# Two recurrent blocks stepped inside the expert slots of the first layer, and the shared expert's last two blocks moved into the second layer's slots

## The chip, the cores and the metric

The kernel runs on one core of one Trainium2 chip. The metric is device time in microseconds (us), the median of the runs shown. Engines: PE (TensorE), DVE (VectorE), ACT (ScalarE), POOL (GpSimd) and SP (SyncE), which here issues most of the DMAs.

## The reference, cut to what matters

`x` has 32 sequences of 128 steps of 128 values, 4,096 tokens. Two layers follow one another, each with a residual sum:

```
z  = polynomial(x, side inputs)                     # per token
x1 = x  + moe0(z)      # 8 experts, top 2, hidden 256, exact gelu, biases
h_t = tanh(x1_t @ Wx + b + h_(t-1) @ Wh)            # 128 steps, one after another
x2 = x1 + shared_swiglu(h) + moe1(h)   # 8 experts, top 2, hidden 256, gates from layernorm(h)
```

All in float32. The recurrence runs over the 128 steps for all 32 sequences at once.

## The kernel before

**Blocks.** Tokens are cut into NB = 8 blocks of 16 steps x 32 sequences (512 tokens, NT = 4 tiles of 128). Each engine has its own instruction stream, written out by hand; order within an engine is program order, and semaphores join the engines.

**Routing of layer 0** goes in five groups of blocks (`GROUPS`). POOL sends each token's row, with its gate and its place, to a region per expert in DRAM (`scatter0`). DVE makes two tables of slots: a first one, of `FULL_SLOTS[0]` = 32 slots that are surely full once the groups up to `CUT` = 2 are counted, and a second with the rest of the 71 slots (`find_blocks`, `sum_table`, `write_table`).

**Slots of layer 0** (`slots0`). A slot is 128 rows of one expert. SP loads its rows from DRAM into a ring of 18 (`slot_rows`; row r waits for the result of slot r-17). In slot j PE does, in this order: transpose rows j+3 (`turn_rows`), the hidden product of j (`hidden_slot`), transpose the activations of j-3 (`turn_act`), and the down product of j-5 (`slot_down`). ACT copies the two transposes and does the gelu; DVE adds the bias and gates the result (`add_bias`, `gate_result`); POOL sends the result rows to DRAM (`send_result`). Each of the four PSUM targets (`up_ps`, `turned_ps`, `act_turned_ps`, `result_ps`) has two banks, used in turn. SP then loads the results back, a block at a time, one after another (`parts`, L466); DVE adds two halves and `x` (`add_one`, `sum_x1`) and gets x1 of the block.

**The recurrent stream** (`stream_body(i)`, i = 0 to 7). Body i does the 16 steps of block i (`rnn_step` on PE, `tanh_step` on ACT) and, between the steps, the work behind block i-1: rows of h transposed and copied for routing (`state_rows`, `copy_rows`), the shared expert (`pair`, `silu`, `multiply`, `down1`), router logits, choice, gates (DVE). In step 10 PE transposes x1 of the next block (`turn_back`) and in steps 13 and 14 multiplies it by Wx (`rnn_input`). The ranks of block i-2 are counted at step 1, and POOL sends its rows from then on, at steps set by `scatter_step`. Body 0 has no block behind it; PE is filled with unused products (`FILL`, `keep_warm`). DVE splits the expert weights into a high and a low part there (`split_wgu`).

**Slots of layer 1** (`slots1`). Four shared slots (`SHARED_SLOTS`) carry the shared expert of block 7, then 71 expert slots follow: the first 40 from table 2, which needs blocks 0 to 5 sent; the other 31 from table 3, which needs all blocks sent. Routing of block 7 is laid between the slots of DVE by `POST_AT`. POOL's queue is: for block 6 eight sends, with the inverse deviation of block 7 (`inv_std`) after three of them; then one result a slot, and the eight sends of block 7 before the results of slots 8 to 15 (`SCATTER_AT`). At the end the result rows are loaded and summed (`add_parts`) and stored.

Of the kernel before, what the change touches and what calls it, by code (L numbers as in the profile page):

```python
# [36 lines left out]
P = 128  # L37
# [9 lines left out]
NG, GT = len(GROUPS), max(len(g) for g in GROUPS) * NT  # L47
# [12 lines left out]
SPLIT = 6  # L60


CUT = 2
ALL_SLOTS, FULL_SLOTS = TOPK * TOK // P + E - 1, (32, 40)
# [5 lines left out]
SHARED_SLOTS = NT  # L70
# [15 lines left out]
for _name, _size in (("ident", P), ("tri", P), ("ones", P), ("center", P), ("ramp", E), ("region", E), ("ids", TOK // P * TOPK),  # L86
                     ("dest", max(LAYER_SLOTS)), ("full", TOK // P), ("whole", TOK // P), ("upto", 4 * E * E), ("slot", max(WIDE)), ("power", NT), ("pad", ROW)):
    CONSTS[_name] = slice(sum(s.stop - s.start for s in CONSTS.values()),
                          sum(s.stop - s.start for s in CONSTS.values()) + _size)
# [11 lines left out]
FILL = [{s: 2 for s in range(STEPS) if s not in (TURN_X1_AT, *XP_AT)}, {1: 2}, {1: 2}] + (NB - 4) * [{}] + [{1: 2, 10: 2}]  # L101
# [3 lines left out]
VAR_STEP = 4  # L105
ONE_AT = {0: (1,), 1: (4,)}, {0: (2, 3), 2: (5,), 3: (6,), 4: (7,)}


def scatter_step(m):

    last = m - (SPLIT - 1) * NT * TOPK
    return 2 * STEPS + 3 + 2 * m if last < 0 else STEPS * (NB - 1) + 1 + 3 * last // 2
# [22 lines left out]
FIRST_X1_AT, FIRST_TURN_AT = 66, ALL_SLOTS + 3  # L135
HELD_ROWS = ALL_SLOTS // ROWS_RING * ROWS_RING + -(-BLK // ROW)
# [6 lines left out]
LAST_STD_BEHIND = 3  # L143


def b_use(n):
    return 2 * n
# [21 lines left out]
def tiles_of(layer, n):  # L169

    return NT if layer else len(GROUPS[n]) * NT


def tiles_on(layer, q, n):

    return sum(tiles_of(layer, m) for m in range(n) if m % (2 + layer) == q)
# [36 lines left out]
def build(nc, consts, x, fside_BxS_0, cond_1024, L0_cond_coeffs, L0_ffn_Wg, L0_ffn_bg, L0_ffn_W1, L0_ffn_b1,  # L213
# [5 lines left out]
    with ExitStack() as ctx:  # L219
# [33 lines left out]
        up_ps, result_ps = banks[:, 0:2, :], banks[:, 2:4, :]  # L253
        turned_ps, act_turned_ps = banks[:, 4:6, :], banks[:, 6:8, :]
# [3 lines left out]
        def rank_ps(layer, n):  # L258
            return bank_b if layer == 0 else turned_ps[:, RANKS_ROW % 2, :] if n == NB - 1 else bank_c
# [7 lines left out]
        last_logits = sb("last_logits", [P, NT * E])  # L267
# [25 lines left out]
        def temporaries(d):  # L293
            buf = work[:, 0, :] if d >= 2 else stream[:, :]
# [9 lines left out]
        stats, moments = sb("stats", [P, NT, 6]), sb("moments", [P, NT, 2])  # L304
        var, rstd = sb("var", [P, NT]), sb("rstd", [P, NT])
        hrows = [hrow0, hrow1]
        ids = const["ids"].rearrange("p (n t k) -> p n t k", n=NB, k=TOPK)
        poss = [[sb(f"pos{k}{q}", [P, (GT, NT)[k], TOPK], U32) for q in range(2 + k)] for k in range(2)]
        pos_f = sb("pos_f", [P, GT, TOPK])
        choices, new_choices = sb("choices", [P, E]), sb("new_choices", [P, E])  # L310
        before = [sb(f"before{q}", [P, NT, E]) for q in range(2)]
# [5 lines left out]
        rows = [next(carve(buf, (ROWS_RING, ROW))) for buf in (hT[:, BLK:], wgu)]  # L317
# [42 lines left out]
        def counted_after(layer, n):  # L360
            return layer and {SPLIT - 1: 1, NB - 1: 2}.get(n)
# [17 lines left out]
        def _(sp):  # L379
# [12 lines left out]
            def slot_rows(d, middle=lambda: None):  # L392
# [65 lines left out]
            slot_rows(1)  # L458
            for n in range(NB):
                if n == 0:  # L460
                    results_landed(0, DONE[0])
                elif n == GROUPS[CUT][-1] + 1:
                    results_landed(0, LAYER_SLOTS[0])
                if n:
                    sp.wait_ge(parts0_in, 16 * n)
                sp.dma_start(parts[:, n, :, :], result_rows[0][n]).then_inc(parts0_in, 16)  # L466
# [1176 lines left out]
```

## Time and profile before

| what | us |
|---|---|
| median of 3 runs (456.72 to 459.83) | 458.12 |
| the profiled execution, device time | 460.27 |
| its span in the profile | 458.5 |
| PE busy / POOL busy / DVE busy in the span | 404.3 / 282.4 / 337.9 |
| granted TensorE clock, mean share of full speed | 0.909 |

The span is what the trace covers; 1.8 us of the device time lie around it. A group of instructions is named by engine, line of the kernel and operands: `L1258` is the helper `mm` that issues every matmul, `L1262` the helper `turn` that issues blocks of transposes, so these are told apart by their operands. `PEld` is the load of weights into the array, which overlaps the products. In brackets stands how long the engine sat idle before and what released it; "issue" means nothing that the profile shows.

### The profile page before, as it was taken

The numbers are of one execution on the slowest core, as the hardware profiler recorded it, in microseconds if no ns is written. First come the engines' busy times: TensorE is split into PE (matmuls) and PEld (weight loads), VectorE is DVE, ScalarE is ACT, GpSimd is POOL, SyncE is SP. The second block draws the span as 40 slices with busy tenths as digits, with TensorE's granted clock in tenths as the row PEclk, the third lists the DMA queues.
The fourth block names the chain that finished last, engine by engine and source line by source line (L and its number), as shares of the span: only waits on it lengthen the run. The fifth ranks groups of instructions, "written<-read, shape, count | busy, mean of one in ns | idle before, by whom it ended". The sixth has DMA issues, their size and how long they took to land.

```text
span 458.5 us, 10143 instructions
## 1 busy us (share of the span) xinstructions
PE 404.3 (88%) x2428; PEld 328.4 (72%) x2428; DVE 337.9 (74%) x1299; ACT 206.4 (45%) x660; POOL 282.4 (62%) x289
## 2 busy tenths in 40 slices
PE   3699889677999999999999999998886999999950
PEld 3376555565899999966878888875675888888840
DVE  4687878388788888883767776888679777667782
ACT  1111304131777777744454554453433455555520
POOL 0536767677777777773146666665445677776670
PEclk9977766557999999999899999998989999999995
DMA  5996111115454444642101111112412353333757
GB/s 146 273 319 213 52 46 54 48 54 126 131 134 109 110 110 108 196 141 87 68 24 37 43 41 36 47 36 76 103 47 70 83 147 96 100 97 84 277 163 211
DMA packets 48150, 49.79 MB, mean 109 GB/s; under 512 B 8627, under 2 KB 37246, under 8 KB 47966
## 3 DMA queue, kind: packets, MB, share of 16 engines
q1 hardware_dynamic: 38680, 30.46, 24.9%
q0 software_dynamic: 8640, 17.84, 11.7%
q10 hardware_dynamic: 774, 0.84, 0.6%
q8 instruction: 23, 0.38, 0.3%
q14 instruction: 33, 0.27, 0.2%
HBM read 27.99 MB, written 21.12 MB: 107 GB/s over the span
## 4 chain that ended last, share of the span: by engine, by line
PE 70%; DVE 16%; DMA 6%; issue 5%; POOL 1%; SPq 1%; ACT 1%; DVEq 0%; POOLq 0%; ACTq 0%
PE banks L1258 58%; PE banks L1262 9%; DMA parts<-results 4%; PE banks L1347 3%; POOL results L541 1%; DMA base<-in_x 1%; DVE stream L802 1%; DVE stream L798 1%; DVE state_lo L1131 1%; DVE stream L796 1%; DVE y_row L1040 1%; DMA results<-y_row,y_dest 0%; DVE stream L793 0%; DVE act_row L1138 0%; DVE rt_d L851 0%
## 5 line engine op out<-in xcount | busy, mean ns | idle before, releaser
L541 POOL DMA_INDIRECT results<-y_row,y_dest x142 | 139.8, 984 | 61.9 <-issue 31.7
L508 POOL DMA_INDIRECT regions<-first_w,pos x64 | 62.1, 971 | 46.7 <-ACT hT L641 29.9
L508 POOL DMA_INDIRECT regions<-parts,pos x64 | 64.2, 1003 | 32.2 <-issue 32.2
L641 ACT ACTIVATE hT<-banks,pcol 128x32 f32<-128x32 f32 x128 | 36.9, 288 | 54.1 <-PE banks L1258 52.6
L623 ACT COPY act_col<-banks 128x256 f32<-128x256 f32 x146 | 54.1, 370 | 10.8 <-PE banks L1262 10.1
L700 ACT ACTIVATE silu_row<-banks 128x256 f32<-128x256 f32 x75 | 28.8, 384 | 63.2 <-PE banks L1258 63.2
L1262 PE MATMUL banks<-const_sb,act_row 128*128 128x128 f32 x292 | 56.6, 276 | 0.0
L1258 PEld LDWEIGHTS banks<-hT,wh 128*128 128x128 f32 x256 | 40.0, 191 | 23.0 <-ACT hT L641 19.4
L1262 PEld LDWEIGHTS banks<-const_sb,act_row 128*128 128x128 f32 x292 | 41.6, 143 | 19.0 <-issue 1.6
L1138 DVE TENSOR_TENSOR act_row<-silu_row,banks 128x256 f32<-128x256 f32 x75 | 31.5, 421 | 29.3 <-ACT silu_row L700 25.9
L1258 PE MATMUL banks<-hT,wh 128*128 128x32 f32 x256 | 50.4, 279 | 0.0
L1258 PE MATMUL banks<-first_w,state 128*128 x142 | 43.7, 391 | 2.0 <-DVE silu_row L1025 1.6
L1258 PE MATMUL banks<-wd,act_col 128*128 x284 | 44.1, 278 | 1.0 <-DVE y_row L1040 1.0
L1258 PE MATMUL banks<-first_w,act_col 128*128 x284 | 43.8, 277 | 0.4 <-ACT act_col L623 0.3
L1258 PE MATMUL banks<-hT,sw_raw 128*128 128x256 f32 x112 | 39.0, 431 | 0.0
L1258 PEld LDWEIGHTS banks<-wd,act_col 128*128 128x128 f32 x284 | 37.7, 193 | 1.4 <-issue 1.3
L1258 PEld LDWEIGHTS banks<-first_w,act_col 128*128 128x128 f32 x284 | 37.3, 191 | 1.3 <-issue 1.2
L617 ACT ACTIVATE act_row<-silu_row 128x256 f32<-128x256 f32 x71 | 29.6, 417 | 14.1 <-DVE silu_row L1025 10.7
L1258 PE MATMUL banks<-parts,xpow 96*128 96x512 f32 x48 | 35.3, 897 | 0.0
L1258 PE MATMUL banks<-wgu_hi,state_hi 128*128 x71 | 34.5, 486 | 0.7 <-issue 0.3
L1025 DVE TENSOR_TENSOR silu_row<-banks,first_w 128x256 f32<-128x256 f32 x71 | 29.7, 419 | 5.9 <-issue 3.7
L1258 PE MATMUL banks<-wgu_hi,state_lo 128*128 x71 | 28.4, 400 | 0.0
(191 smaller groups left out, 831.7 us busy)
## 6 DMA issues: line engine op xcount, KB each, us to landing
parts<-results SPq DMA_DIRECT2D x16, 512.0 KB, 5.6
hT<-regions SPq DMA_DIRECT2D x71, 65.0 KB, 1.8
wgu<-regions SPq DMA_DIRECT2D x71, 65.0 KB, 1.9
results<-y_row,y_dest POOLq DMA_INDIRECT x142
base<-in_x SPq DMA_DIRECT2D x12, 128.0 KB, 3.2
out<-base SPq DMA_DIRECT2D x20, 64.0 KB
regions<-const_sb SPq DMA_DIRECT2D x18, 65.0 KB
first_w<-in_L_ffn_W SPq DMA_DIRECT2D x1, 1024.0 KB, 8.3
```

The costliest lines, as they stand in the source:

```text
L508: pool.indirect_dma_start(regions[layer], bass.IndirectOffsetOnAxis(ap=poss[layer][q][:, t, k:k + 1], axis=0), hrows[layer][:, q, t, k, :] ...
L541: pool.indirect_dma_start(results[layer], bass.IndirectOffsetOnAxis(ap=y_dest[:, s:s + 1], axis=0), y_row[:, s, :], None).then_inc(results ...
L617: nc.scalar.activation(act_row[:, j % ACT_RING, :], silu_row[:, j % SILU_RING, :], ACT.Gelu).then_inc(slot_act[0], 1)
L623: nc.scalar.copy(act_col[:, j % ACT_RING, :], act_turned_ps[:, j % 2, 0:HID]).then_inc(act_copied[layer], 1)
L641: nc.scalar.activation(hT[:, hcols(n, step_col(s), B)], rnn_ps[:, p, step_col(s):step_col(s) + B], ACT.Tanh, bias=pcol[:, ROW_CB:ROW_CB + ...
L700: nc.scalar.activation(silu_row[:, q % SILU_RING, :], up_ps[:, q % 2, 0:HID], ACT.Silu).then_inc(slot_silu, 1)
L796: dve.tensor_tensor(zt, p1, zt, ALU.add).then_inc(poly_taken, 1)
L1025: dve.tensor_tensor(silu_row[:, j % SILU_RING, :], up_ps[:, j % 2, 0:HID], b1[:, bass.ds(e * HID, HID)], ALU.add).then_inc(biased, 1)
L1138: dve.tensor_tensor(act_row[:, q % ACT_RING, :], silu_row[:, q % SILU_RING, :], up_ps[:, q % 2, HID:2 * HID], ALU.mult).then_inc(slot_act[ ...
L1258: return nc.tensor.matmul(dst, w, v, start=start, stop=stop, **kw)
L1262: ins = nc.tensor.transpose(bank[:, t * P:(t + 1) * P], tile, ident)
L1347: nc.tensor.transpose(turned_ps[:, r % 2, 0:P], rows[layer][:, s, 0:D], ident).then_inc(turned[layer], 1)
```

## The change

- The 32 steps of blocks 0 and 1 are issued inside `slots0`, from slot 46 on, one in a slot and two in each fourth slot (`steps_in_slot`). In slot j the step stands on PE behind the hidden product, a second one at the slot's end; on ACT the tanh stands behind the copy of the transposed rows. `turn_back(0)` stands at slot 44, `rnn_input(0)` at slot 45; those of blocks 1 and 2 follow the steps.
- Stream bodies run for i = 2 to 7 and carry the work behind block i-2 (`LAG` = 2). The filler products of bodies 0 to 2 are gone.
- So that banks are left for the recurrence, layer 0's slots have one bank each for transposed rows, transposed activations and results; only the hidden product keeps two.
- `CUT` = 1 and `FULL_SLOTS[0]` = 16, so that blocks 0 to 2 are complete after 31 slots. SP loads the results of block 0, 1 and 2 beside rows 54, 60 and 64; DVE adds `x` at slots 41, 50 and 61 and makes x1 at 43, 52 and 63. Blocks 3 to 7 are loaded when all results have landed.
- The layer-0 row ring lies in `wgu_lo`, not in `hT`, so the split of the weights moves to POOL, three experts behind the last result of layer 0 and five behind the inverse deviation of block 0. ACT and PE wait for all 71 results before block 0's rows are transposed and copied.
- Blocks 6 and 7 share one routing round of eight tiles, and both go through shared slots: eight in place of four. `POST_AT` moves by two slots. Block 5's ranks come at step 15 of body 7, and its positions, the counting of blocks and table 2 behind them on DVE.
- POOL's queue in layer 1: the eight sends of block 5 behind the stream, with the inverse deviation of the late round after three of them; then the 16 sends of blocks 6 and 7, one each before the results of slots 8 to 23.

```diff
+LATE = tuple(range(SPLIT, NB))
+ROUNDS = GROUPS, tuple((n,) for n in range(SPLIT)) + (LATE,)
+GT = max(len(blocks) for rounds in ROUNDS for blocks in rounds) * NT
+LAST_ROUND = len(ROUNDS[1]) - 1
-CUT = 2
-ALL_SLOTS, FULL_SLOTS = TOPK * TOK // P + E - 1, (32, 40)
+CUT = 1
+ALL_SLOTS, FULL_SLOTS = TOPK * TOK // P + E - 1, (16, 40)
-SHARED_SLOTS = NT
+SHARED_SLOTS = len(LATE) * NT
-FILL = [{s: 2 for s in range(STEPS) if s not in (TURN_X1_AT, *XP_AT)}, {1: 2}, {1: 2}] + (NB - 4) * [{}] + [{1: 2, 10: 2}]
+FILL = {1: 2, 10: 2}
+LAG = 2
-POST_AT = {"logits": 3, "one": 4, "two": 5, "gates": 8, "rows": 9, "ranks": 11, "blocks": 14, "slots": 16}
-SCATTER_AT, PADS_AT = [0] * NT * TOPK + list(range(NT * TOPK, 2 * NT * TOPK)), (20, 32)
+POST_AT = {"logits": 5, "one": 6, "two": 7, "gates": 10, "rows": 11, "ranks": 13, "blocks": 16, "slots": 18}
+SCATTER_AT, PADS_AT = list(range(NT * TOPK, 3 * NT * TOPK)), (12, 32)
+EARLY_BLOCKS = LAG
+LOAD_AT, X1_AT = {54: 0, 60: 1, 64: 2}, {43: 0, 52: 1, 63: 2}
+TURN_FIRST_AT, FIRST_STEP_AT = 44, 46
+EARLY_ROWS_AT, EARLY_COPIES_AT = 10, (11, 12)
+def steps_in_slot(j):
+    return 0 if j < FIRST_STEP_AT else 1 + ((j - FIRST_STEP_AT) % 4 == 2) if j < ALL_SLOTS else 1
+LAST_STD_BEHIND, SPLIT_FIRST = 3, 3
...
+        def result_of(layer, q):
+            return banks[:, 2 + q % 2, 0:D] if layer else bank_b[:, 0:D]
+        def turned_of(layer, r):
+            return banks[:, 4 + r % 2, 0:P] if layer else banks[:, 2, 0:P]
+        def act_turned_of(layer, q):
+            return banks[:, 6 + q % 2, 0:HID] if layer else banks[:, 3, 0:HID]
...
 # SP, in slot_rows
                     if r >= ROWS_RING:
                         sp.wait_ge(y_ready[layer], layer * SHARED_SLOTS + r - ROWS_RING + 1)
+                    beside(r)
...
 # POOL
+            def split_wgu(e):
+                pool.wait_ge(wgu_cast, e + 1)
+                cols_e = slice(e * 2 * HID, (e + 1) * 2 * HID)
+                pool.tensor_tensor(wgu_lo[:, cols_e], wgu[:, cols_e], wgu_hi[:, cols_e].bitcast(F32), ALU.subtract).then_inc(wgu_split, 1)
             for r in range(LAYER_SLOTS[0]):
                 send_result(0, r)
+            for e in range(SPLIT_FIRST):
+                split_wgu(e)
...
+            for i in range(NT * TOPK):
+                if i == LAST_STD_BEHIND:
+                    inv_std(LAST_ROUND)
+                scatter1(m + i)
             for r in range(LAYER_SLOTS[1]):
                 for i, at in enumerate(SCATTER_AT):
                     if at == r:
-                        if i == LAST_STD_BEHIND:
-                            inv_std(NB - 1)
                         scatter1(SPLIT * NT * TOPK + i)
                 send_result(1, r)
 # DVE, in slots0
+                    if j + 2 in X1_AT:
+                        add_one(X1_AT[j + 2])
+                    if j in X1_AT:
+                        sum_x1(X1_AT[j])
 # DVE, stream_body, after gates(1, n, n % 3)
+                if n == SPLIT - 1:
+                    positions(1, n, n % 3)
                     find_blocks(2)
+                    make_table(2)
 # PE, the waits on what is now one bank
-                if r >= 2:
-                    pe.wait_ge(state_ready[layer], r - 1)
+                if r >= 1 + layer:
+                    pe.wait_ge(state_ready[layer], r - layer)
...
-                if j >= 2:
-                    pe.wait_ge(y_ready[layer], j - 1)
+                if j >= 1 + layer:
+                    pe.wait_ge(y_ready[layer], j - layer)
 # PE, in slots0
                         hidden_slot(j, experts[j])
+                    if until > done:
+                        early_step(done)
                     if 0 <= j - act_lag < count:
                         turn_act(0, j - act_lag)
                     if j >= lag:
                         slot_down(0, j - lag, w2, experts.pop(j - lag) * HID)
+                    if until > done + 1:
+                        early_step(done + 1)
+            def early_step(t):
+                i, s = divmod(t, STEPS)
+                rnn_step(i, i % 2, s)
+                if s == TURN_X1_AT:
+                    turn_back(i + 1)
+                if s in XP_AT:
+                    rnn_input(i + 1, (i + 1) % 2, XP_AT.index(s))
-            for i in range(NB):
+            for i in range(LAG, NB):
                 stream_body(i, i % 2)
```

## Rows read from the trace of the kernel before

**Rows 1.** The page, the chain that ended last, its shares by engine.

```profile
PE 70%; DVE 16%; DMA 6%; issue 5%; POOL 1%; SPq 1%; ACT 1%; DVEq 0%; POOLq 0%; ACTq 0%
```

**Rows 2.** Windows by stage: length, busy time per engine, clock, DMA share, GB/s.

```profile
116.00:163.00 47.00, 47.00 (x351) 42.98 (x349) 38.03 (x153) 36.08 (x120) 35.59 (x37) 1.00 0.46 119
...
202.00:214.70 12.70, 12.70 (x69) 8.49 (x67) 7.58 (x14) 5.19 (x18) 6.93 (x6) 1.00 0.23 68
214.70:229.60 14.90, 14.90 (x87) 12.29 (x87) 8.94 (x42) 7.13 (x22) 1.42 (x1) 0.89 0.23 76
229.60:243.50 13.90, 13.90 (x93) 11.22 (x92) 10.47 (x49) 7.12 (x22) 6.96 (x7) 1.00 0.08 25
...
298.30:311.30 13.00, 13.00 (x84) 10.03 (x83) 11.28 (x48) 6.66 (x21) 8.41 (x9) 1.00 0.12 37
311.30:322.40 11.10, 8.33 (x35) 4.79 (x33) 8.30 (x43) 4.01 (x12) 6.63 (x7) 0.85 0.37 91
```

**Rows 3.** Timeline of one slot of layer 0 and the start of the next.

```profile
176.63 0.14 PEld L1347 LDWEIGHTS banks<-const_sb,hT 128*128 128x128 f32 x1
...
177.70 0.37 ACT L623 COPY act_col<-banks 128x256 f32<-128x256 f32 x1 [0.23 <-PE banks L1262]
177.84 0.14 PEld L1347 LDWEIGHTS banks<-const_sb,hT 128*128 128x128 f32 x1
...
178.28 0.36 PEld L1262 LDWEIGHTS banks<-const_sb,act_row 128*128 128x128 f32 x2
178.29 0.96 POOL L541 DMA_INDIRECT results<-y_row,y_dest  x1 [0.31 <-issue]
```

**Rows 4.** Timeline of the stream, body 0: a step's weight load and the next.

```profile
204.45 0.30 PEld L1258 LDWEIGHTS banks<-hT,wh 128*128 128x128 f32 x2 [0.26 <-ACT hT L641]
...
204.66 0.30 PEld L1258 LDWEIGHTS banks<-wgu_hi 128*128 128x128 f32 x2
```

**Rows 5.** The chain that ended last in order of time, around the end of layer 0's slots.

```profile
182.28 3.63 DMA parts<-results
...
197.59 0.61 DVE parts L1066
```

**Rows 6.** Timeline of DVE, SP and PE around the stream's end.

```profile
299.56 0.42 DVE L963 TENSOR_TENSOR first_w<-counts,const_sb 128x256 f32<-128x256 f32 x1
...
301.60 0.87 DVE L820 BATCH_NORM_STATS2 stats<-first_w 128x6 f32<-128x128 f32 x4
...
309.41 0.48 DVE L992 TENSOR_TENSOR first_w<-const_sb,ends 128x320 f32<-128x320 f32 x1
...
312.98 0.22 DVE L886 TENSOR_SCALAR rt_den<-rt_th 128x36 f32<-128x36 f32 x1
...
315.90 0.90 SPq L409 DMA_DIRECT2D wgu<-regions  x2
...
318.79 0.87 DVE L820 BATCH_NORM_STATS2 stats<-first_w 128x6 f32<-128x128 f32 x4
...
322.36 0.49 PE L1258 MATMUL banks<-wgu_hi,state_hi 128*128 x1 [0.34 <-issue]
```

**Rows 7.** Timeline of POOL in layer 1's slots, single sends.

```profile
312.99 0.96 POOL L508 DMA_INDIRECT regions<-first_w,pos  x1 [0.43 <-issue]
...
320.37 1.04 POOL L533 TENSOR_TENSOR rstd<-var,const_sb 128x4 f32<-128x4 f32 x1
...
350.96 0.96 POOL L508 DMA_INDIRECT regions<-first_w,pos  x1 [0.30 <-issue]
...
370.44 0.96 POOL L508 DMA_INDIRECT regions<-first_w,pos  x1 [0.30 <-issue]
...
411.35 0.96 POOL L541 DMA_INDIRECT results<-y_row,y_dest  x1 [0.52 <-issue]
...
446.47 0.96 POOL L541 DMA_INDIRECT results<-y_row,y_dest  x1 [0.30 <-issue]
```

More of the change, by code:

```diff
@@ L169, in tiles_of @@
 def tiles_of(layer, n):
-    return NT if layer else len(GROUPS[n]) * NT
+    return len(ROUNDS[layer][n]) * NT
 def tiles_on(layer, q, n):
-    return sum(tiles_of(layer, m) for m in range(n) if m % (2 + layer) == q)
+    return sum(NT if layer else tiles_of(0, m) for m in range(n) if m % (2 + layer) == q)
 class Chain:
@@ L360, in counted_after @@
         def counted_after(layer, n):
[L361 removed]
+            return layer and {SPLIT - 1: 1, LAST_ROUND: 2}.get(n)
         def table_values(eng, d, at, count, most):
@@ L747, in _ @@
             load_tables(ACT.Silu)
-            act.wait_ge(y_ready[0], HELD_ROWS)
-            for i in range(NB):
-                if i == 1:
-                    act.wait_ge(y_ready[0], LAYER_SLOTS[0])
+            for i in range(LAG, NB):
                 stream_body(i, i % 2)
@@ L841, in choose_one @@
+                link(dve.tensor_tensor(logit, logit, per_expert(gate_b1, tiles), ALU.add))
             def choose_one(layer, n):
@@ L868, in choose_two @@
                     now, after = before[n % 2], before[1 - n % 2]
-                    for t in range(NT - 1):
+                    for t in range(tiles - 1):
                         link(dve.tensor_tensor(now[:, t + 1, :], now[:, t, :], mask[:, t, :], ALU.add))
-                    dve.tensor_tensor(after[:, 0, :], now[:, NT - 1, :], mask[:, NT - 1, :], ALU.add).then_inc(chosen_ready[1], 1)
+                    dve.tensor_tensor(after[:, 0, :], now[:, tiles - 1, :], mask[:, tiles - 1, :], ALU.add).then_inc(chosen_ready[1], 1)
                     dve.wait_ge(chosen_ready[1], n + 1)
@@ L1034, in gate_result @@
                 row, y = rows[layer][:, r % ROWS_RING, :], y_row[:, s, :]
-                gate, result = row[:, D:D + 1], result_ps[:, q % 2, 0:D]
+                gate, result = row[:, D:D + 1], result_of(layer, q)
                 if layer == 0:
@@ L1245, in _ @@
             slots0()
-            for i in range(NB):
-                stream_body(i, i % 2)
+            for i in range(LAG, NB):
+                stream_body(i)
             slots1()
@@ L1400, in slots0 @@
                         turn_rows(0, j + AHEAD)
-                    if j == FIRST_TURN_AT:
-                        pe.wait_ge(state_ready[0], count)
+                    if j == TURN_FIRST_AT:
+                        pe.wait_ge(rnn_w_in, 32)
                         turn_back(0)
+                    if j == TURN_FIRST_AT + 1:
+                        for k in range(2):
+                            rnn_input(0, 0, k)
+                    done, until = steps_until(j), steps_until(j + 1)
                     if j < count:
@@ L1440, in slots1 @@
                     if q == 1:
-                        logits1(last, range(NT))
+                        late_logits()
                     if 0 <= q - act_lag < count:
@@ new lines, in stream_body @@
+                    if n and s == RANKS_AT:
+                        ranks1(n - 1)
+                    for c in range(NC):
+                        for part in range(2):
+                            if s in PAIR_AT[c][part]:
+                                pair(n, c, part, PAIR_AT[c][part].index(s))
+                    if s in LOGIT1_AT:
+                        k = LOGIT1_AT.index(s)
+                        logits1(n, (2 * k, 2 * k + 1))
+                    for c in range(NC):
+                        for k in range(2):
+                            if s == DOWN_AT[c][k]:
+                                down1(n, c, (2 * k, 2 * k + 1))
@@ L1608, in _ @@
             slots0()
-            pe.wait_ge(rnn_w_in, 32)
             pe.wait_ge(shared_in, 48)
-            pe.wait_ge(gate1_taken, 1)
-            for k in range(2):
-                rnn_input(0, 0, k)
-            for i in range(NB):
+            for i in range(LAG, NB):
                 stream_body(i, i % 2)
```

365 lines of the change are left out of this document (186 added, 179 removed).

## The prediction

> **What bounds the kernel now.** First the page's chain: 70% of the path is PE, and no other engine has more than 16% [rows 1]. Then the windows by stage, because a mean over stages hides what each is worth [rows 2]. In layer 0's slots PE is busy 47.00 us of 47.00: every instruction put there is paid, unless something else was going to stall. In the stream the reader sees PE "busy" all the time too, but there it is a chain: body 0 takes 12.7 us for 16 steps, 0.79 us each, product, tanh, product. Between the stream and the expert slots of layer 1 lies a seam of 11.1 us in which PE is busy for 8.33 at a clock of 0.85. Last the timelines: a slot of layer 0 takes 1.21 us (176.63 to 177.84), POOL needs 0.31 + 0.96 = 1.27 us for a send [rows 3], and in layer 1's slots POOL runs behind until the send at 411.35, the first that starts in step with the slots, 0.52 + 0.96 = 1.48 us apart [rows 7]. So POOL, off the chain today, has little room there. I call E the stream's end (311.3) and S the first expert product of layer 1 (322.36, E + 11.1) [rows 2, 6].
>
> **What it removes.** Bodies 0 and 1, 12.7 + 14.9 = 27.6 us [rows 2], from the path.
>
> **What comes into layer 0's slots.** (a) A step occupies PE for 0.21 us, the distance from its weight load to the next one (204.45 to 204.66) [rows 4]; 32 steps, PE full: +6.7. (b) Three `turn_back` and six `rnn_input` lay in PE's gaps of the stream and now lie in full slots: an estimate of 12 transposes at 0.14 us and 12 products at 0.2: +4.1. (c) In the six double slots the next step waits for a tanh that stands behind a gelu: 0.15 us each, +0.9 (0 to 2). (d) The load of block 0 stands beside row 54, which waits for result 36; DVE makes that at slot 41, and its next act there is `add_one(0)`, which needs the load. A load takes 3.63 us [rows 5], SP about 0.9 before it (twelve waits, an estimate). DVE stands for 4.5 us, with `add_bias` and `gate_result` behind it; PE gets about one microsecond further and waits at a down product, since the single result bank must be read first. With the add itself: +5.3 (2 to 7). Then `turn_back(0)` at slot 44 waits for `sum_x1(0)`, which DVE does behind slot 43's result: +1.4 (0 to 2). The other loads have 3 and 10 slots' time and are hidden. (e) After the idle PE runs at the lower of its two levels for a while, as in the seam (0.85 in place of 1.00 over 11.1 us is 1.7 us) [rows 2]: +1.7 (0 to 2). (f) One bank instead of two: ACT's copy ends at 178.07 and PE reloads that bank from 178.28 [rows 3]. 0.2 us of slack hold in the steady slot and go where DVE reads its table, each fourth slot: +1.5, between 0 and 18 x 0.2 = 4. (g) Table 1 grows from 40 to 56 slots, table 0 shrinks: +0.4. (h) Two adds of 0.6 to 0.7 us leave DVE's tail [rows 5]: -1.3. Sum: 6.7 + 4.1 + 0.9 + 5.3 + 1.4 + 1.7 + 1.5 + 0.4 - 1.3 = +20.7. Body 2 begins 27.6 - 20.7 = 6.9 us earlier.
>
> **The stream.** Body 2 is now the one that starts cold, with block 0 behind it, x1 of block 3 loaded only after the last result has landed, and logits behind that add: I give it body 1's 14.9 for its 13.9 [rows 2], +1.0 (-1 to +3). The others keep their length. The split of the weights costs POOL eight operations that no row shows there; between the 0.7 us of a large DVE add and twice POOL's 1.04 for a tiny one [rows 7] I take 1.2. It hides behind body 2, where POOL has nothing to send; without that cover 10 us would be late. E comes 5.9 earlier.
>
> For this the Trainium skill has a rule (SBUF — State Buffer, "Who interferes with whom"): a DVE operation with two SBUF inputs and a GpSimd operation that reads SBUF cannot overlap, and the later one waits out the whole instruction. The rows above show no such pair. By the rule the adds for x1 of block 3 could wait for one split, and the sum below would be 1.2 us longer.
>
> **The seam: a new wait.** Block 5's ranks now come at the last step. Behind them DVE has positions 1.1 us, counting blocks 2.04 (299.56 to 301.60) and table 2 3.57 (309.41 to 312.98) before it may multiply shared slot 0 [rows 6]: at E + 7.4; before, E + 4.6. From there to the variance operations it is 2.9 us (315.90 to 318.79) [rows 6], and these now cover eight tiles, 2.6 us: E + 12.9. POOL has sent three of block 5's rows and stands at `inv_std`, which needs that variance, with the other five sends queued behind it. So 1.04 us for it, then five sends at 1.27 [rows 3, 7]: the last ends at about E + 20.4. SP's first row of table 2 waits for all of block 5: before, it followed the last send's end by 1.95 us (313.95 to 315.90) [rows 6, 7], so now E + 22.4. From row to first expert product it was 6.5 us with PE busy, and at least 3; PE will be waiting, so I take 3.9: E + 26.3, against E + 11.1: **+15.2** (12 to 19). Four shared slots and the longer variance alone would have brought about +9.4; the rest is the wait.
>
> **The last stage.** Before, POOL began the late sends at 350.96, S + 28.6, which is twelve slots of 1.48 and about 10 us of routing stalls [rows 7]. Now S + 28, the choice having moved into the shared slots. Sixteen sends are paired with results, 2.53 us a pair, where there were eight: the last starts at S + 66.3 (before 370.44, S + 48.1) and ends at S + 67.3. Row 40, the first of table 3, can leave 1.95 later and is there at about S + 71. PE asks for it at S + 37 x 1.48 + 10 = S + 65: a stall of 6. From S + 67.6 POOL still has 47 sends before the last, 59.7 us: S + 127.3, and the restarted PE is no faster. I take S + 128 against 446.47, S + 124.1 [rows 7]: +3.9 (0 to 7). What follows stays.
>
> **Sum.** -5.9 + 15.2 + 3.9 = **+13.2**. The profiled execution's span would be 471.7 and its device time, with the 1.8 us around the span, 473.5; it lay 2.1 us above the median of the runs. On the median: 458.1 + 13.2 = **471.3 us**, slower by 2.9%.
>
> **Rivals.**
> 1. *Not slower: the steps ride free.* If PE's busy time in the slots is only how the trace draws pipelined products, a slot with a step still takes 1.21 us and DVE's wait at slot 41 is taken up by slack. Then a to e, 20.1 us, are gone: 471.3 - 20.1 = 451.2. It decides from where a slot with one step stays below 1.25 us. Against it: the weight loads alone are 42.98 of 47.00 us [rows 2], and slots follow one another at one distance. 0.11.
> 2. *The load wait at slot 41 is hidden*, because SP is ahead or the banks let PE run on: d and e go, 8.4 us: 462.9. Against it stands that the load cannot leave before result 36. 0.14.
> 3. *Row 40 comes in time*, since the seam's stall lets POOL draw level: 467.4. For it: POOL idles in the seam. Against: the pairs begin only at slot 8's result. 0.13.
> 4. *The single banks bind in every slot*, by 0.2 us: 71 x 0.2 = 14 in place of 1.5: 483.8. 0.10.
> The forecast has 0.52, with 464 to 478 as its own range.
>
> **How the numbers follow.** A measurement of this kernel tells about 1% from no change, so "same" is 453.5 to 462.7. Rival 1 is faster save a little: 0.10. Half of rival 2 and the rest of rival 1 make "same": 0.13 with the forecast's low end. Slower: 0.77. The range of 8 in 10 goes from 459 to 480; below it lies rival 1, above it most of rival 4.
>
> **What would show it.** Right: slots from 46 on at 1.4 to 1.5 us, 1.6 to 1.7 when double; DVE idle for about 4.5 us before `add_one(0)`, released by the load of `parts`; the last `split_wgu` on POOL before body 3; DVE at table 2 until about 7 us after the stream; `inv_std` of the last round with five sends behind it, and SP's first row of table 2 about 22 us after the stream's end; late sends of POOL for 38 us in pairs; a PE gap at expert slot 37 released by rows. Wrong: the first expert product less than 20 us after the stream's end, no gap at slot 37, or body 2 starting before 217.

## The result, and the profile after

| | before | after |
|---|---|---|
| median, us | 457.42 (454.40 to 460.54, 6 runs) | 517.20 (513.82 to 520.68, 6 runs) |
| ratio | 1 | 1.130 (95%: 1.122 to 1.137) |
| profiled execution, us | 460.27 | 513.82 |
| its span, us | 458.5 | 512.0 |

Slower, as forecast, but by 60 us and not by 13. In some executions a kernel runs some per cent slower at a lower granted clock; medians and ranges here are of all executions, ratios and their intervals leave the slow ones out. The two profiled executions are 53.5 us apart and not 60, since that of before is above its median and that of after is the fastest of its six. The page's chain:

```profile
PE 61%; DVE 21%; issue 7%; DMA 6%; POOL 2%; ACT 1%; DVEq 1%; SPq 1%; POOLq 0%; ACTq 0%
```

PE carries 61% of the path where it carried 70 [rows 1]; DVE went from 16 to 21%. PE now waits for others. Where it waits, the windows by stage say (length, then busy time of PE, PEld, DVE, ACT and POOL, then granted clock, DMA share, GB/s):

```profile
124.00:170.00 46.00, 38.94 (x230) 29.16 (x230) 25.41 (x101) 26.95 (x77) 24.07 (x26) 1.00 0.28 74
...
225.00:251.00 26.00, 20.96 (x140) 16.96 (x139) 13.90 (x54) 14.56 (x45) 13.40 (x14) 0.97 0.11 37
252.60:266.60 14.00, 13.94 (x52) 12.77 (x53) 8.48 (x20) 5.49 (x17) 12.76 (x10) 0.50 0.37 123
...
271.20:285.20 14.00, 14.00 (x96) 11.37 (x94) 11.22 (x54) 7.29 (x23) 7.13 (x7) 1.00 0.22 68
338.80:367.80 29.00, 18.70 (x76) 11.80 (x75) 15.76 (x71) 6.80 (x21) 11.58 (x11) 0.78 0.14 39
```

The first row is the surprise: long before the first step (slot 46) PE is busy for 38.94 of 46 us in slots that took 47.00 of 47.00 before [rows 2]. The other rows are the last slots, body 2 at half the clock (0.50), body 3, and the seam, 29 us for 11.1. A slot from the timeline, early in the stage, shows what PE waits for:

```profile
129.56 0.71 PE L1328 MATMUL banks<-first_w,act_col 128*128 x4 [0.32 <-DVE y_row L1124]
...
130.43 0.29 DVE L1121 TENSOR_TENSOR y_row<-banks,first_w 128x128 f32<-128x128 f32 x1 [0.78 <-PE banks L1328]
130.75 0.16 DVE L1123 TENSOR_TENSOR y_dest<-wgu_lo,const_sb 128x1 uint32<-128x1 f32 x1
130.83 0.28 DVE L1124 TENSOR_SCALAR y_row<-y_row,wgu_lo 128x128 f32<-128x128 f32 x1
...
131.36 0.71 PE L1328 MATMUL banks<-first_w,act_col 128*128 x4 [0.33 <-DVE y_row L1124]
```

It is a closed loop: down product 0.71 us, handing over from PE to DVE 0.16, the three operations of `gate_result` to 131.11 (0.68), and 0.25 until PE starts the next down product, which may not start before DVE has signalled that it is done with the single result bank: 1.80 us for a slot, against 1.21 [rows 3]. The groups by line give the total:

```profile
L1121 DVE TENSOR_TENSOR y_row<-banks,first_w 128x128 f32<-128x128 f32 x71 | 20.7, 291 | 49.7 <-PE banks L1328 49.7
```

Over layer 0's 71 slots DVE stood idle for 49.7 us before that one operation (9.2 us before its counterpart, L1037, in the kernel before). The distance stays the same where the slots carry steps:

```profile
226.02 0.29 DVE L1121 TENSOR_TENSOR y_row<-banks,first_w 128x128 f32<-128x128 f32 x1 [0.65 <-PE banks L1328]
227.82 0.29 DVE L1121 TENSOR_TENSOR y_row<-banks,first_w 128x128 f32<-128x128 f32 x1 [0.18 <-PE banks L1328]
229.61 0.29 DVE L1121 TENSOR_TENSOR y_row<-banks,first_w 128x128 f32<-128x128 f32 x1 [0.78 <-PE banks L1328]
```

1.80 and 1.79 us, with one step in each; the next distance, to 231.41, holds two steps and is 1.80 as well. The steps lie in the hole that the loop leaves.

The time by stages, both from the profiled executions (the mark of each is its first step, first expert product or last send):

| up to | before | after | difference so far | this stage | forecast |
|---|---|---|---|---|---|
| body 2 starts | 229.6 | 251.8 | +22.2 | +22.2 | -6.9 |
| stream ends (E) | 311.3 | 338.8 | +27.5 | +5.3 | +1.0 |
| first expert product (S) | 322.4 | 367.8 | +45.5 | +18.0 | +15.2 |
| last send starts | 446.5 | 500.2 | +53.7 | +8.2 | +3.9 |
| end of span | 458.5 | 512.0 | +53.5 | -0.2 | 0 |

Of the 40 us between forecast and result 29 arise in the slots of layer 0.

### The profile page after: what moved, and what is told of

It is laid out like the page before. It is cut to its first block, busy times and chain, and to the rows that moved or that the text cites. A ratio compares the mean times of both kernels' runs of the same rounds, so it can differ in the third digit from the quotient of the medians.

```text
span 512.0 us, 10060 instructions
## 1 busy us (share of the span) xinstructions
PE 422.4 (82%) x2394; PEld 335.3 (65%) x2394; DVE 333.3 (65%) x1264; ACT 212.1 (41%) x665; POOL 290.7 (57%) x296
## 4 chain that ended last, share of the span: by engine, by line
PE 61%; DVE 21%; issue 7%; DMA 6%; POOL 2%; ACT 1%; DVEq 1%; SPq 1%; POOLq 0%; ACTq 0%
PE banks L1328 51%; PE banks L1332 8%; PE banks L1418 2%; DVE y_row L1124 2%; DMA regions<-first_w,pos 2%; DVE y_row L1121 2%; DMA parts<-results 2%; DVE stream L874 1%; DVE stream L870 1%; DVE stream L868 1%; POOL regions L553 1%; DVE stream L865 1%; DMA base<-in_x 1%; DMA wgu<-regions 1%; POOL results L593 1%
## 5 line engine op out<-in xcount | busy, mean ns | idle before, releaser
L593 POOL DMA_INDIRECT results<-y_row,y_dest x142 | 137.4, 967 | 120.8 <-DVE y_row L1124 101.3
L1328 PE MATMUL banks<-first_w,act_col 128*128 x284 | 50.6, 302 | 19.7 <-DVE y_row L1124 17.2
L1332 PE MATMUL banks<-const_sb,act_row 128*128 128x128 f32 x300 | 59.9, 282 | 0.0
L1207 DVE TENSOR_TENSOR act_row<-silu_row,banks 128x256 f32<-128x256 f32 x79 | 33.1, 421 | 40.7 <-ACT silu_row L775 38.0
L1332 PEld LDWEIGHTS banks<-const_sb,act_row 128*128 128x128 f32 x300 | 43.4, 151 | 19.8 <-issue 4.6
L1328 PEld LDWEIGHTS banks<-hT,wh 128*128 128x128 f32 x256 | 44.6, 203 | 17.4 <-ACT hT L713 12.7
L1121 DVE TENSOR_TENSOR y_row<-banks,first_w 128x128 f32<-128x128 f32 x71 | 20.7, 291 | 49.7 <-PE banks L1328 49.7
L1328 PE MATMUL banks<-first_w,state 128*128 x142 | 45.8, 406 | 1.6 <-ACT state L670 0.8
L1109 DVE TENSOR_TENSOR silu_row<-banks,first_w 128x256 f32<-128x256 f32 x71 | 29.9, 421 | 10.7 <-PE banks L1328 10.3
L1328 PE MATMUL banks<-hT,sw_raw 128*128 128x256 f32 x96 | 36.1, 461 | 0.0
L1418 PE MATMUL banks<-const_sb,wgu 128*128 128x128 f32 x71 | 21.1, 297 | 17.8 <-DMA wgu<-regions 11.7
## 6 DMA issues: line engine op xcount, KB each, us to landing
parts<-results SPq DMA_DIRECT2D x16, 512.0 KB, 3.7
```

The source lines that it names most:

```text
L593: pool.indirect_dma_start(results[layer], bass.IndirectOffsetOnAxis(ap=y_dest[:, s:s + 1], axis=0), y_row[:, s, :], None).then_inc(results ...
L1109: dve.tensor_tensor(silu_row[:, j % SILU_RING, :], up_of(0, j), b1[:, bass.ds(e * HID, HID)], ALU.add).then_inc(biased, 1)
L1121: link(dve.tensor_tensor(y, result, b2[:, bass.ds(e * D, D)], ALU.add))
L1207: dve.tensor_tensor(act_row[:, q % ACT_RING, :], silu_row[:, q % SILU_RING, :], up_of(1, q)[:, HID:2 * HID], ALU.mult).then_inc(slot_act[1 ...
L1328: return nc.tensor.matmul(dst, w, v, start=start, stop=stop, **kw)
L1332: ins = nc.tensor.transpose(bank[:, t * P:(t + 1) * P], tile, ident)
```

## The experiments

The question was what makes a slot 1.8 us long. Theory A is the loop above. Theory B is the other single banks, those of the transposed rows and activations, from which the prediction's step (f) and its rival 4 had read their slack. A third possibility was the steps. The distance of a slot is the mean between the first and the last send of POOL from 135 to 165 us of each trace (17 to 24 sends), which includes the reads of the table. Where slots are short (the kernel before, `e5_rings_while_free`) it is POOL's own pace, 0.30 us idle and 0.96 a send, and PE's slot is a little shorter.

| kernel | us | slot, us |
|---|---|---|
| before | 457.2 | 1.27 |
| changed | 517.2 | 1.84 |
| `e1_two_result_banks` | 506.0 | 1.57 |
| `e2_before_one_result_bank` | 500.6 | 1.83 |
| `e3_bank_free_after_add` | 495.6 | 1.47 |
| `e4_before_one_transposed_bank` | 465.2 | 1.30 |
| `e5_rings_while_free` | 485.5 | 1.26 |

**The result bank alone, in the kernel before.**

```diff
-                if j >= 2:
-                    pe.wait_ge(y_ready[layer], j - 1)
+                if j >= 1 + layer:
+                    pe.wait_ge(y_ready[layer], j - layer)
```

> The kernel before, with one edit: in layer 0 each down product waits until the result before it is gated, as if it had one bank. Theory A: slots at 1.79 in place of 1.21 us, 0.58 x 71 = 41 us more, 457 + 41 = about 498. Theory B: no change, 457.

Measured: 500.56 us (499.34 to 503.82), ratio 1.097 (1.092 to 1.102): +43 us from one wait. Its timeline has the loop of the changed kernel, 1.79 us from one down product to the next:

```profile
150.94 0.71 PE L1258 MATMUL banks<-first_w,act_col 128*128 x4 [0.33 <-DVE y_row L1040]
...
151.80 0.29 DVE L1037 TENSOR_TENSOR y_row<-banks,first_w 128x128 f32<-128x128 f32 x1 [0.78 <-PE banks L1258]
...
152.73 0.71 PE L1258 MATMUL banks<-first_w,act_col 128*128 x4 [0.33 <-DVE y_row L1040]
```

**The transposed banks alone, in the kernel before.**

```diff
-                if r >= 2:
-                    pe.wait_ge(state_ready[layer], r - 1)
+                if r >= 1 + layer:
+                    pe.wait_ge(state_ready[layer], r - layer)
...
-                if j >= 2:
-                    pe.wait_ge(act_copied[layer], j - 1)
+                if j >= 1 + layer:
+                    pe.wait_ge(act_copied[layer], j - layer)
```

> The kernel before, with one bank's waits for the transposed rows and the transposed activations of layer 0, and two result banks as they were. Theory A and step (f) of the prediction: +0 to 4 us, 457 to 461. Theory B: the whole 41 us, about 498.

Measured: 465.23 us (462.26 to 470.43), ratio 1.015 (1.009 to 1.021), so +4 to +10. In the profiled executions its span is 3.7 us longer and body 0 starts 3.7 us later (205.85 for 202.13). Theory B's 498 did not come: these banks are not the main cause. Step (f), sized from them at 1.5 (0 to 4), came out at its upper end or above it.

**Two banks for the results, one for the hidden product.**

```diff
-            return banks[:, q % 2, :] if layer else banks[:, q % 2, 0:HID]
+            return banks[:, q % 2, :] if layer else banks[:, 0, 0:HID]
-            return banks[:, 2 + q % 2, 0:D] if layer else bank_b[:, 0:D]
+            return banks[:, 2 + q % 2, 0:D] if layer else banks[:, 7 - 6 * (q % 2), 0:D]
...
-                if j >= 2:
-                    pe.wait_ge(biased, j - 1)
+                if j >= 1:
+                    pe.wait_ge(biased, j)
...
-                if j >= 1 + layer:
-                    pe.wait_ge(y_ready[layer], j - layer)
+                if j >= 2:
+                    pe.wait_ge(y_ready[layer], j - 1)
```

> In the changed kernel, layer 0's results get two banks again and the hidden product gives one up (its reader, the bias add, comes early in DVE's slot). Theory A, the loop through the single result bank (down product 0.71 us, three DVE operations, next down product) sets every slot at 1.79 us: slots without a step go back to 1.21 to 1.27 us, 0.55 x 46 = 25 us saved there; the 25 slots with steps become PE-bound at 1.45, 8 us saved; the wait for block 0's load stays. 517 - 33 = about 484. Theory B, the single transposed banks or the steps are what holds the slots: slots stay at 1.79 and the time at 517. Theory C, the single bank of the hidden product binds instead: between the two.

Measured: 505.98 us (504.56 to 507.49). Theory A's number (484) was missed and theory C came, a time between the two: the single bank moved to the hidden product makes a loop of its own.

```profile
159.88 0.69 PE L1328 MATMUL banks<-first_w,state 128*128 x2
...
160.74 0.43 DVE L1109 TENSOR_TENSOR silu_row<-banks,first_w 128x256 f32<-128x256 f32 x1 [0.17 <-PE banks L1328]
...
161.41 0.69 PE L1328 MATMUL banks<-first_w,state 128*128 x2
```

0.69 for the product, 0.17, 0.43 for the add of the bias, 0.24: 1.53 us. I had called this reader early and so harmless; what counts is the length of the loop, not the reader's place in DVE's slot.

**The bank free after its only reader.** The add of b2 (L1121) reads the bank; the other two operations don't.

```diff
-                    link(dve.tensor_tensor(y, result, b2[:, bass.ds(e * D, D)], ALU.add))
+                    dve.tensor_tensor(y, result, b2[:, bass.ds(e * D, D)], ALU.add).then_inc(result_taken, 1)
+                    dve.wait_ge(result_taken, r + 1)
...
-                    pe.wait_ge(y_ready[layer], j - layer)
+                    pe.wait_ge(*((y_ready[1], j - 1) if layer else (result_taken, j)))
```

> The changed kernel, with the single result bank declared free by the first of DVE's three operations (the add of b2, the only one that reads the bank) and not by the last. Theory A: the loop loses two operations, some 0.4 us, so slots at about 1.4 us; 46 x 0.4 = 18 us, and in the slots with steps 25 x 0.33 = 8: 517 - 26 = about 491. Theory B: no change, 517.

Measured: 495.60 us (493.81 to 500.14), 22 us less than the changed kernel, slots at 1.47: the loop by its own arithmetic, 0.71 + 0.16 + 0.29 + 0.25 = 1.41. In its trace the down products are 1.40 us apart, and 1.62 and then 1.31 around each read of the table. Theory A had said 491.

**Second banks for as long as they are idle.** The recurrence needs its three banks only from slot 44 on. On top of the last edit:

```diff
+ROWS_TWO, ACTS_TWO, RESULTS_TWO = 44, 40, 49
-            return banks[:, 2 + q % 2, 0:D] if layer else bank_b[:, 0:D]
+            return banks[:, 2 + q % 2, 0:D] if layer else banks[:, 6 if q % 2 and q < RESULTS_TWO else 7, 0:D]
-            return banks[:, 4 + r % 2, 0:P] if layer else banks[:, 2, 0:P]
+            return banks[:, 4 + r % 2, 0:P] if layer else banks[:, 4 if r % 2 and r < ROWS_TWO else 2, 0:P]
-            return banks[:, 6 + q % 2, 0:HID] if layer else banks[:, 3, 0:HID]
+            return banks[:, 6 + q % 2, 0:HID] if layer else banks[:, 5 if q % 2 and q < ACTS_TWO else 3, 0:HID]
...
+                back = 1 if layer or j < RESULTS_TWO else 0
+                if j >= 1 + back:
+                    pe.wait_ge((result_taken, y_ready[1])[layer], j - back)
```

The waits for the other two rings are changed in the same way.

> The changed kernel; the three single rings of layer 0 (transposed rows, transposed activations, results) get their second bank back for as long as the recurrence doesn't need it (rows to 43, activations to 39, results to 48), and the single result bank is free after the add of b2. Theory A: slots to about 45 at 1.21 to 1.25 us, 45 x 0.55 = 25 us; the slots with steps, PE-bound or bound by the single bank at 1.45, 25 x 0.34 = 8 us: 517 - 33 = about 484; if the steps cost more in a full slot than 0.21 us each, up to 492. Theory B, that something other than the rings makes the slots long in this kernel (rows in the other memory, the earlier tables): the time stays above 500.

Measured: 485.46 us (484.34 to 485.73), 31.7 us less than the changed kernel; the down products are 1.21 us apart again, so the rows in the other memory and the earlier tables cost the slots nothing that shows:

```profile
150.09 0.61 PE L1331 MATMUL banks<-first_w,act_col 128*128 x4
...
151.30 0.61 PE L1331 MATMUL banks<-first_w,act_col 128*128 x4
```

This trace also prices the steps in slots without the long loop. The first step starts at 173.58, the 32nd at 214.09, 25 slots later: 40.5 us, where 25 slots at 1.21 take 30.3. So +10.3 for 31 steps, two `turn_back` and four `rnn_input`; steps (a) to (c) of the prediction give 6.7 + 0.9 + two thirds of 4.1 = 10.3. The single result bank's 1.4 us still lies in these slots, so this is a sum that fits rather than a proof of each term.

**The terms (d), seam and last stage, one edit after another,** each on top of the kernel above it.

```diff
-LOAD_AT, X1_AT = {54: 0, 60: 1, 64: 2}, {43: 0, 52: 1, 63: 2}
+LOAD_AT, X1_AT = {50: 0, 60: 1, 64: 2}, {43: 0, 52: 1, 63: 2}
```

> As the one above, with the load of block 0's results issued beside row 50 in place of 54, so four slots earlier. Theory A (step (d) of the prediction): DVE's wait of 4 us before the add for block 0 goes, and with it most of the gap on PE: 4 to 6 us less than the kernel above. Rival: the load waits for the results' sends to land and not for its row, so it leaves no earlier, and less than 1.5 us is won.

Measured: 481.11 us (479.94 to 482.37), 4.4 less. The add of block 0 in this kernel, and in the one before it:

```profile
161.04 0.69 DVE L1154 TENSOR_TENSOR parts<-base,parts 128x512 f32<-128x512 f32 x1 [1.62 <-DMA parts<-results]
```

```profile
163.83 0.69 DVE L1154 TENSOR_TENSOR parts<-base,parts 128x512 f32<-128x512 f32 x1 [3.83 <-DMA parts<-results]
```

```diff
             for i in range(NT * TOPK):
-                if i == LAST_STD_BEHIND:
-                    inv_std(LAST_ROUND)
                 scatter1(m + i)
+            inv_std(LAST_ROUND)
```

> As the one above, with the inverse deviation of the late round behind all eight sends of block 5 on POOL, in place of behind three. Theory (the prediction's seam): the five sends no longer wait for a variance over eight tiles; the last of them ends about 7 us earlier, and so do SP's first row of table 2 and the first expert product: 5 to 7 us less. Rival: table 2 or the landing of the sends holds the rows anyway, and less than 2 us is won.

Measured: 475.27 us (473.50 to 475.92), 5.8 less. POOL and SP in this kernel; the last send before the deviation, the deviation, and the first rows of table 2:

```profile
318.51 0.96 POOL L555 DMA_INDIRECT regions<-first_w,pos  x1 [0.30 <-issue]
...
320.63 1.67 POOL L581 TENSOR_TENSOR rstd<-var,const_sb 128x8 f32<-128x8 f32 x1 [1.17 <-DVE var L900]
```

```profile
321.01 25.89 SPq L449 DMA_DIRECT2D wgu<-regions  x23
```

The rows leave before the deviation is done, at 321.01, where the kernel with the earlier load had them at 328.76; its first expert product comes at 328.01 for 333.20.

```diff
-SCATTER_AT, PADS_AT = list(range(NT * TOPK, 3 * NT * TOPK)), (12, 32)
+SCATTER_AT, PADS_AT = [4 + i // 2 for i in range(2 * NT * TOPK)], (12, 32)
```

> As the one above, with the 16 late sends two each before results 4 to 11, in place of one each before results 8 to 23. Theory (the prediction's last stage): they end 10 us or more earlier, so row 40 is there when PE asks for it and the gap at expert slot 37 (6 us predicted) goes: 3 to 6 us less. Rival: POOL is the bound of the stage from there on, so its last send comes at the same time, and less than 1.5 us is won.

Measured: 466.62 us (465.58 to 468.47), 8.7 less, more than the 3 to 6 expected: in the profiles 6.0 us lie between the first expert product and the last send, and 2.2 before it, which this edit does not explain. PE's waits from 340 us on lose the one on row 40, which was 6.9 us long in the kernel without this edit:

```profile
PE banks L1421 <- DMA wgu<-regions: 6.9, 1, 6.9
PE banks L1421 <- DVE state_lo L1202: 4.8, 2, 3.3
```

and here:

```profile
PE banks L1421 <- DVE state_lo L1202: 4.9, 2, 3.3
PE banks L1330 <- DVE y_row L1126: 0.9, 1, 0.9
```

**The start of the stream.** Body 2 ran at half the clock. In the changed kernel it comes behind the drain, the last down products, before each of which PE idles:

```profile
248.97 0.75 PE L1328 MATMUL banks<-first_w,act_col 128*128 x4 [1.09 <-DVE y_row L1124]
...
250.81 1.22 PE L1328 MATMUL banks<-first_w,act_col 128*128 x4 [1.08 <-DVE y_row L1124]
```

So unused products were put into these gaps, two behind each of the last five down products.

```diff
+                    if j >= count:
+                        for _ in range(DRAIN_FILL):
+                            mm(banks[:, 2, :], wgu_hi[:, 0:P], wgu_hi[:, 0:2 * HID])
```

> As the kernel with denser late sends (466.6 us), with two unused products of 512 columns behind each of the last five down products of layer 0, where PE idles 0.7 us of every 1.4. Theory: the first block of the stream then starts at the full clock (0.53 over 14.4 us in the kernel without them) and takes 0.8 us a step in place of 1.28: 4 to 6 us less, 461 to 462. Rival: the block is held by ACT and the loads and not by the clock, or the products only delay the down products: within 1 us of 466.6.

Measured: 468.22 us (467.51 to 472.06), ratio to before 1.028 (1.021 to 1.034) where the kernel with denser sends had 1.024 (1.018 to 1.031): no gain, and not the 461 to 462 that was expected. The clock did come: 1.00 over the first steps of body 2 (219.2 to 227.6), where it was 0.54 (217.6 to 230.1). But the transposes of block 3's x1 start no earlier, first without the products and then with them:

```profile
230.10 1.09 PE L1334 MATMUL banks<-const_sb,base 128*128 128x128 f32 x4
```

```profile
229.92 0.69 PE L1335 MATMUL banks<-const_sb,base 128*128 128x128 f32 x4 [2.37 <-DVE base L1159]
```

Then the drain's results in idle banks, the load at row 49, x1's transposes a slot later:

```diff
-TURN_FIRST_AT, FIRST_STEP_AT = 44, 46
+TURN_FIRST_AT, FIRST_STEP_AT = 45, 46
+DRAIN_RESULTS = ALL_SLOTS - 4
-LOAD_AT, X1_AT = {50: 0, 60: 1, 64: 2}, {43: 0, 52: 1, 63: 2}
+LOAD_AT, X1_AT = {49: 0, 60: 1, 64: 2}, {43: 0, 52: 1, 63: 2}
...
+            return banks[:, 2 + q % 2, 0:D] if layer else banks[:, q % 2 if q >= DRAIN_RESULTS else 6 if q % 2 and q < RESULTS_TWO else 7, 0:D]
```

> As the one above, with the last four results in the two banks of the hidden product, which are free by then, the load of block 0 beside row 49, and the transposes of its x1 a slot later (45). Expected: each of the last four down products 0.3 to 0.6 us closer, the waits of 1.2 us for the load and 1.2 us for x1 mostly gone: 2 to 4 us less than the one above. Rival: ACT's copies hold the drain at the same distance and the load only leaves later for the sends to land: less than 1 us.

Measured: 468.74 us (464.99 to 473.05), ratio 1.024 (1.016 to 1.033): the 2 to 4 us expected can't be told from nothing. Then eight products before the late logits:

```diff
+                        for _ in range(SEAM_FILL):
+                            mm(banks[:, 5, :], wgu_hi[:, 0:P], wgu_hi[:, 0:2 * HID])
                         late_logits()
```

> As the one above, with eight unused products on PE before the late logits, where it waits 2 to 3 us for ACT's copy. Theory: the shared slots then run at the full clock (0.76 over 14 us before) and the first expert product comes 1 to 2 us earlier: about 457 or less, level with or a little faster than the kernel before. Rival: block 5's eight sends and the first row of table 2 set that product, so nothing is won, or up to 1 us is lost.

Measured: 467.04 us (461.04 to 472.24), ratio 1.022 (1.017 to 1.028), and not about 457: again within the scatter, which is 5 to 11 us in these three kernels and 1 to 3 us in the four before them. In its profile the first expert product does come 4.2 us earlier (322.22 for 326.39) and the late logits take 1.95 us for 3.58; but that execution (461.04 us) is the fastest of six, and the medians don't bear out a gain. The same profile shows what bounds the start of the stream. Windows over the first steps of body 2, its gap, and the steps behind it:

```profile
214.60:222.90 8.30, 7.85 (x47) 5.74 (x45) 4.16 (x12) 4.31 (x13) 7.55 (x8) 1.00 0.28 90
222.90:226.80 3.90, 0.56 (x6) 0.53 (x6) 3.09 (x4) 0.77 (x2) 3.90 (x3) 1.00 0.45 149
226.80:234.70 7.90, 7.90 (x36) 7.03 (x35) 7.11 (x28) 2.03 (x7) 3.00 (x3) 0.57 0.41 133
```

The clock is 1.00 and ten steps follow one another at 0.79 us, and then PE stands:

```profile
226.28 0.66 PE L1337 MATMUL banks<-const_sb,base 128*128 128x128 f32 x4 [3.34 <-DVE base L1161]
```

The transposes of block 3's x1 wait for its load, which leaves only when the last result of layer 0 has landed. With the slow clock the steps were late and hid this wait; with the fast one it shows, and behind it the granted clock is 0.57. What the steps gained, the wait took back. Twelve products more in front of that wait, to hold the clock:

```diff
                         if s == TURN_X1_AT:
+                            for _ in range(WAIT_FILL if i == LAG else 0):
+                                mm(rnn_ps[:, 1 - p, :], wgu_hi[:, 0:P], wgu_hi[:, 0:2 * HID])
                             turn_back(i + 1)
```

> As the kernel with filled seam (467.0 us, 461.0 to 472.2 in six runs), with twelve unused products in front of the transposes of block 3's x1, where PE waits 3.3 us for them. Theory: the steps behind that wait run at 0.8 us and not at 1.3 to 2.1, so about 3 us less, 464. Rival: the whole start of the stream is bound by the load of block 3, which leaves when the last result has landed, and the clock lost behind it is a small part: less than 1.5 us.

Measured: 466.17 us (463.63 to 473.07), ratio to before 1.020 (1.015 to 1.025): 0.9 us less than 467.04, which is the rival's figure and within the scatter. No version reached the kernel before; the best are 2% behind it, and which waits make up these last 2% was not tested.

## Why the prediction was wrong

**What it removes** (27.6 us) held: the two bodies are gone.

**Step (f), one bank instead of two, is the step that failed,** and with it rival 4. Both read the slack off ACT's copy of the transposed activations, 0.2 us [rows 3], and never asked the same of the result bank. The trace of before had the answer in the same slot:

```profile
177.50 0.61 PE L1258 MATMUL banks<-first_w,act_col 128*128 x4
...
178.27 0.29 DVE L1037 TENSOR_TENSOR y_row<-banks,first_w 128x128 f32<-128x128 f32 x1 [0.19 <-PE banks L1258]
...
178.67 0.28 DVE L1040 TENSOR_SCALAR y_row<-y_row,hT 128x128 f32<-128x128 f32 x1
...
178.71 0.61 PE L1258 MATMUL banks<-first_w,act_col 128*128 x4
```

The next down product starts at 178.71, before the gating ends at 178.95. With one bank it waits for that gating and for the 0.25 us of handing back: at least 1.70 us from product to product by these rows. The loop takes 1.8 us where a slot took 1.21: 0.58 x 71 = 41 us, priced at 1.5. Rival 4 had the right effect, "the single banks bind in every slot", but from the same slack: 0.2 us for 0.58, and a chance of 0.10. The kernel before with that one wait alone is 43 us slower. Even the two transposed banks were 4 to 10 us and not 1.5. (The 178.28 of the forecast is the load of the array; the transposes that write a bank start at 178.49.)

**Steps (a) to (c), 11.7 us,** fit a full slot, as `e5_rings_while_free` suggests, but cost nothing in the changed kernel: a slot that waits 0.6 us for the loop takes a step for nothing. So rival 1's "steps ride free" came true as well, by luck, for a reason that it did not have. Loop, less the steps and what (f) allowed: 41.2 - 11.7 - 1.5 = 28.0 of the 29.1 us missed in this stage.

**Step (d)** was right. The prediction had DVE standing 4.5 us before `add_one(0)`, PE a little less at a down product, and 1.4 us for `turn_back(0)`. (A row r waits for r - 17 results, that is for slot r - 18: 36 for row 54, as the prediction has it, and not r - 17 as in the section on the kernel before.)

```profile
185.87 0.69 DVE L1151 TENSOR_TENSOR parts<-base,parts 128x512 f32<-128x512 f32 x1 [4.12 <-DMA parts<-results]
...
187.73 0.95 PE L1328 MATMUL banks<-first_w,act_col 128*128 x4 [4.28 <-DVE y_row L1124]
...
190.26 1.09 PE L1332 MATMUL banks<-const_sb,base 128*128 128x128 f32 x4 [1.37 <-DVE base L1156]
```

Four rows earlier was worth 4.4 us, so rival 2 falls. Of (e) the last of these rows shows the lower clock: four transposes in 1.09 us, which take 0.64 in body 3. The clock was 0.53 from 187.7 to 194.5, with PE busy for 5.39 us of it; that is an estimate of 2.5 us for the 1.7.

**The stream, +1.0, was +5.3.** Body 2 takes 19.3 us (251.81 to 271.15), not 14.9. Its clock was 0.50 for 14 of these, behind a drain in which PE idled for about half of each slot; with the gaps filled it was 1.00. But where the clock was held, the wait for x1 of block 3 took its place, so this stage had two bounds close together, and its price can't be laid on the clock alone. The adds for x1 met the splits of the weights on POOL. The prediction had allowed 1.2 us for this and left it out of the sum:

```profile
259.46 7.06 POOL L585 TENSOR_TENSOR wgu_lo<-wgu,wgu_hi 128x512 fp32r<-128x512 f32 x5
...
259.86 1.41 DVE L1151 TENSOR_TENSOR parts<-base,parts 128x512 f32<-128x512 f32 x1 [1.51 <-DMA parts<-results]
261.30 1.64 DVE L1156 TENSOR_TENSOR base<-parts 128x512 f32<-128x512 f32 x1
262.86 0.68 DVE L1165 TENSOR_TENSOR first_w<-first_w,banks 128x512 f32<-128x512 f32 x1
```

The two adds take 3.05 us where they take 1.37 in slots 41 to 43 (0.69 and 0.68): +1.7. The third operation has the same size and one input in PSUM, and keeps its 0.68 us beside the same splits. The Trainium skill (SBUF — State Buffer, "Who interferes with whom") states that a DVE instruction with two SBUF inputs contends with a GpSimd instruction that reads SBUF, and one with a single SBUF input, outside DVE's two-port modes, does not; the trace agrees, 1.41 and 1.64 against 0.68 us. No run took the splits away.

**The seam, +15.2, was +18.0,** by the chain described:

```profile
346.29 0.32 DVE L1098 CAST table<-first_w 128x40 int32<-128x40 f32 x1
...
354.01 1.67 POOL L579 TENSOR_TENSOR rstd<-var,const_sb 128x8 f32<-128x8 f32 x1 [7.41 <-DVE var L899]
...
361.00 0.96 POOL L553 DMA_INDIRECT regions<-first_w,pos  x1 [0.30 <-issue]
363.51 5.69 SPq L447 DMA_DIRECT2D wgu<-regions  x10
...
367.84 0.79 PE L1328 MATMUL banks<-wgu_hi,state_hi 128*128 x1 [0.17 <-DVE state_lo L1200]
```

E is 338.8: table 2 done at E + 7.8 (forecast 7.4), the deviation starts at E + 15.2 (12.9), the last send ends at E + 23.2 (20.4), rows at E + 24.7 (22.4), product at E + 29.0 (26.3). 2.3 of the 2.7 us are lost before the variance, in a wait that the prediction did not have:

```profile
344.00 1.07 ACT L729 COPY first_w<-banks 128x512 f32<-128x512 f32 x2 [5.64 <-DMA regions<-first_w,pos]
...
345.13 3.58 PE L1328 MATMUL banks<-wgate1c,hT 128*128 128x8 f32 x16 [3.34 <-ACT first_w L729]
```

ACT's copy of late rows waits for sends of an earlier block to land, PE waits for the copy, and then does the late logits at a clock of 0.50 (346.4 to 351.4); DVE, in order, reaches the variance behind the shared slot that follows, 5.0 us after table 2 where the prediction took 2.9 from before. Taking the deviation out of the sends' way gave 5.8.

**The last stage, +3.9, was +8.2.** Late sends in pairs 2.53 us apart, and the gap at row 40 as forecast (5.4 for 6):

```profile
441.02 0.47 PE L1418 MATMUL banks<-const_sb,wgu 128*128 128x128 f32 x1 [5.39 <-DMA wgu<-regions]
```

The prediction let POOL's queue set the end from S + 67 on, so that PE's pause would partly vanish behind it. But POOL drew level with the slots at 479.82, 20 us before its last send, and waited for them over the next 10 us. Denser sends shortened the stage from S to the last send from 132.1 us (460.10 - 328.01) to 126.1 (451.95 - 325.85): of the pause of 6.9 us 6.0 had been paid. Rival 3 falls, since row 40 did not come in time.

## What to carry to other kernels

When a ring is cut from two buffers to one, write the loop out for each ring: producer, handing over, every operation up to the signal that frees the buffer, handing back. If that is longer than the step's period, the difference is paid in every step, however small the slack of the neighbours looks; and check which operation is the buffer's last reader, since signalling there is free (22 us here, in the changed kernel). A new loop also makes whatever is put into its gaps look free, so costs and gains of two edits must not be added before the loop is known. And before filling gaps to hold the clock, ask what else is late there: here the faster steps only ran into a load.

## What was not expected of the hardware

- A down product of 0.71 us and a following DVE read are 0.87 us apart from start to start, and PE starts again 0.25 us after DVE's last operation ends: 0.4 us of the 1.8 us loop are handing over alone.
- A DVE add of 128x512 with both inputs in SBUF took 1.41 and 1.64 us beside POOL's subtractions, 0.69 alone; with an input in PSUM it took 0.68 beside them.
- The TensorE clock was granted at 1.00 throughout slots in which PE was busy for 38.94 of 46.00 us, and at 0.50 (the lower level, 1.2 GHz) in body 2, behind four down products 1.8 us apart with 0.87 to 1.09 us of idle before each.
